# Experts stage: the two expert slots of a token are joined before the down-projection

## The reference, cut to what matters

```python
probs = softmax(x @ gate_w.T)                 # 8 experts
vals, idx = top_k(probs, 2)                   # two "slots" of each token
rw = vals / sum(vals)                         # weight of slot 0 and of slot 1
d1 = (x A1[e]) B1[e] * 2;  d3 = (x A3[e]) B3[e] * 2        # adapters of rank 16
act = silu(x w_gate + d1) * (x w_up + d3)     # per expert, 512 wide
out = (sum over e of weight * act) @ w_down.T
out = out + sum over e of weight * (act A2[e]) B2[e] * 2
```

## Time and profile before

| | |
|---|---|
| median of 3 runs | 1726.71 us (1726.4 to 1728.2) |
| time of the profiled execution | 1729.46 us |
| span of the profiled execution | 1727.7 us |
| PE busy | 1639.9 us (95%) |
| DVE busy | 1239.3 us (72%) |
| ACT busy | 926.0 us (54%) |
| POOL busy | 879.3 us (51%) |
| mean granted TensorE clock | 0.961 of full speed |

### The profile page before, as it was taken

The page is one execution under the profiler, slowest core; times in us unless marked ns, Lnnn a source line. Parts: engine busy times, 40 slices in busy tenths (PEclk is TensorE's granted clock), DMA queues, the critical chain, the costliest instruction groups (busy, mean ns, idle before and its releaser), DMA issues. The chain is left out here.

```text
span 1727.7 us, 42620 instructions
## 1 busy us (share of the span) xinstructions
PE 1639.9 (95%) x14336; PEld 1227.0 (71%) x14336; DVE 1239.3 (72%) x2888; ACT 926.0 (54%) x2189; POOL 879.3 (51%) x1006
## 2 busy tenths in 40 slices
PE   5999999999978999999999999897999999999998
PEld 2555555555545666666666666556999999999998
DVE  5887777777745767777676777536878788787876
ACT  3554444555533666666665666645554555455453
POOL 3544444444435767777766677622434334343442
PEclk9999999999977989999998999988999999999999
DMA  4000000000000000000000000000000000000000
GB/s 122 13 3 2 1 1 1 1 1 1 2 9 3 6 7 6 7 7 6 7 7 7 6 7 5 16 30 1 8 9 9 6 9 6 9 8 8 9 6 13
DMA packets 27869, 16.62 MB, mean 10 GB/s; under 512 B 6193, under 2 KB 25586, under 8 KB 27762
## 3 DMA queue, kind: packets, MB, share of 16 engines
q1 hardware_dynamic: 27762, 15.23, 3.2%
HBM read 9.97 MB, written 4.19 MB: 8 GB/s over the span
## 5 line engine op out<-in xcount | busy, mean ns | idle before, releaser
L323 ACT ACTIVATE sa_P<-sa_SK 128x1024 f32<-128x1024 f32 x128 | 131.2, 1025 | 149.0 <-PE sa_SK L514 149.0
L1554 POOL TENSOR_TENSOR ff_zz<-ff_zt 128x256 f32<-128x256 f32 x32 | 37.5, 1170 | 318.4 <-DVE ff_zt L1758 318.4
L278 POOL TENSOR_TENSOR sa_KM<-sa_HQK,sc_headmask 128x512 fp32r<-128x512 f32 x64 | 66.6, 1040 | 249.3 <-ACT sa_HQK L318 249.3
L963 ACT ACTIVATE xa_P<-xa_SK 77x1024 f32<-77x1024 f32 x128 | 130.1, 1016 | 95.0 <-PE xa_SK L1286 94.8
L1622 ACT ACTIVATE ff_SG<-bank 128x512 f32<-128x512 f32 x128 | 76.6, 598 | 188.7 <-PE bank L1835 188.7
L1748 DVE TENSOR_TENSOR ff_GL<-ff_GU,ff_GH 128x512 fp32r<-128x512 f32 x128 | 148.4, 1178 | 27.2 <-ACT ff_GH L1627 27.2
L408 DVE TENSOR_REDUCE sa_mx<-sa_SQ 128x8 f32<-128x1024 f32 x128 | 156.5, 1223 | 7.8 <-PE sa_SQ L514 5.4
L1900 PE MATMUL bank<-fh_r,ff_GH 128*128 128x256 f32 x512 | 149.3, 292 | 0.0
L889 POOL TENSOR_TENSOR xa_QMH<-xa_QBH,xc_headmask 128x512 fp32r<-128x512 f32 x64 | 72.6, 1134 | 148.0 <-ACT xa_QBH L953 147.9
L1833 PE MATMUL bank<-ff_ZH,fh_b 128*128 128x256 f32 x512 | 146.0, 285 | 0.0
L1902 PE MATMUL bank<-fh_r,ff_GL 128*128 128x256 f32 x512 | 144.5, 282 | 0.0
(11 more groups left out here) (259 smaller groups left out, 5394.7 us busy)
## 6 DMA issues: line engine op xcount, KB each, us to landing
xa_shift<-xa_row SPq DMA_DIRECT2D x256, 2.0 KB
out<-X SPq DMA_DIRECT2D x64, 64.0 KB, 1.5
cx<-ctx SPq DMA_DIRECT2D x64, 38.5 KB
sa_shift<-sa_mT SPq DMA_DIRECT2D x64, 8.0 KB, 1.8
X<-x SPq DMA_DIRECT2D x1, 768.0 KB, 6.4
xa_E<-L_ffn_B SPq DMA_DIRECT2D x2, 256.0 KB, 3.6
xa_E<-down_a SPq DMA_DIRECT2D x1, 512.0 KB, 4.3
X<-x SPq DMA_DIRECT2D x1, 256.0 KB, 2.9
```

The costliest lines, as they stand in the source:

```text
L323: nc.scalar.activation(P[:, 2 * (k % 2) + h, :], SK[:], ACT.Exp).then_inc(p_ready, 1)
L963: nc.scalar.activation(P[0:TC, (2 * b + h) % 4, :], SK[0:TC, :], ACT.Exp).then_inc(p_ready, 1)
```

## The change

Six edits, all within the experts:

1. **Slots joined.** The output is divided by the weight of slot 0: unit 2 and 3 (slot 1) are scaled by the ratio of the two weights, added to units 0 and 1, and only then split and projected down. POOL `scaled` multiplies the silu of slot 1 by the ratio; DVE `slot_sum` adds.
2. **The ratio.** DVE `odds` makes it, PE `ratios` spreads it over all 128 rows (two float32 matmuls of 128 columns), ACT `ratio_copy` brings it to the tile RB.
3. **Down-projection turned round.** `down` now has the weights stationary and 256 tokens as moving columns. The third adapter (bank PZ) is computed from slot 0's units and from the sums; the down-projection itself (bank OUT) from the sums alone.
4. **Masked adapter parts.** DVE `z_parts` masks the two with M0 - (M0 + M1) and M0 + M1, which POOL `output_masks` makes; ACT `z_hi` and DVE `z_lo` split both parts (128 by 512 in all), `extra` adds both to OUT. ACT `out_copy`, PE `back_T` and DVE `residual` bring the result back with tokens as rows.
5. **`x_lo` goes from DVE to POOL**, to the head of POOL's step. The comparisons in `ranks` become a function `compare` of two instructions instead of four, `second` and `slot_weights` go.
6. **Order.** New orders in `step` on PE, ACT, DVE and POOL, and the matching waits.

```diff
 @@ pool
-            def slot_sum(g):
-                pool.wait_ge(zt_done, NB * g + NB)
-                need(pool, zT_ps, g)
-                nc.gpsimd.tensor_tensor(zz[:], zt[:, :, 0, :], zt[:, :, 1, :], ALU.add).then_inc(zz_done, 1)
+            def slot_inputs(g, p, s):          # two of the four products as before, for one slot
...
+            def x_lo(g, p):
+                pool.wait_ge(xh_ready, g + 1)
+                need(pool, up_ps, UNITS * (g - 2) + 2)
+                nc.gpsimd.tensor_tensor(XX[1][:, p, :], xT[:], XX[0][:, p, :].bitcast(F32), ALU.subtract).then_inc(xl_ready, 1)
+            def output_masks(g, p):
+                pool.wait_ge(mask_sb, g + 1)
+                need(pool, zb_done, 2 * (g - 1))
+                nc.gpsimd.tensor_tensor(ME[:, p, 1], M[:, 0, :], M[:, 1, :], ALU.add).then_inc(me_done, 1)
+                pool.wait_ge(me_done, 2 * g + 1)
+                nc.gpsimd.tensor_tensor(ME[:, p, 0], M[:, 0, :], ME[:, p, 1], ALU.subtract).then_inc(me_done, 1)
+            def scaled(g, u):
+                pool.wait_ge(rb_sb, g + 1)
+                pool.wait_ge(silu_done, UNITS * g + 2 + u + 1)
+                unit2 = SG[:, u, :].rearrange("f (c n) -> f c n", c=2)
+                nc.gpsimd.tensor_tensor(unit2, unit2, RB[:].unsqueeze(1).to_broadcast([128, 2, NT]),
+                                        ALU.mult).then_inc(scaled_done, 1)
             def step(g, p):
-                if real(g - 1):
-                    slot_sum(g - 1)
                 if real(g + 1):
-                    slot_inputs(g + 1, 1 - p)
+                    x_lo(g + 1, 1 - p)
+                    slot_inputs(g + 1, 1 - p, 0)
+                scaled(g, 0)
+                scaled(g, 1)
+                if real(g + 1):
+                    slot_inputs(g + 1, 1 - p, 1)
+                    output_masks(g + 1, 1 - p)
 @@ act, step
                 if real(g + 1):
                     a_hi(g + 1)
+                ratio_copy(g)
...
                 silu(g, 2)
-                silu(g, 3)
                 if real(g - 1):
                     z_hi(g - 1)
-                g_hi(g, 2)
-                g_hi(g, 3)
+                silu(g, 3)
                 if real(g + 2):
                     input_T(g + 2, p)
+                g_hi(g, 2)
+                if real(g - 1):
+                    out_copy(g - 1)
+                g_hi(g, 3)
 @@ dve
+            def odds(g):
+                dve.wait_ge(w0_ready, g + 1)
+                nc.vector.reciprocal(w0_inv[:], W0[:, bass.ds(NB * g, NB)]).then_inc(inv_ready, 1)
+                dve.wait_ge(inv_ready, g + 1)
+                dve.wait_ge(w1_ready, g + 1)
+                need(dve, rb_ps, g)
+                nc.vector.tensor_tensor(ratio[:], w1[:], w0_inv[:], ALU.mult).then_inc(ratio_ready, 1)
             def gated(g, k):
-                dve.wait_ge(silu_done, UNITS * g + k + 1)
+                if k < 2:
+                    dve.wait_ge(silu_done, UNITS * g + k + 1)
+                else:
+                    dve.wait_ge(scaled_done, 2 * g + k - 1)
...
+            def slot_sum(g, u):
+                dve.wait_ge(gu_done, UNITS * g + 2 + u + 1)
+                nc.vector.tensor_tensor(GU[:, u, :], GU[:, u, :], G1[:, u, :], ALU.add).then_inc(sum_done, 1)
+            def z_parts(g, p):
+                dve.wait_ge(y_ps, UNITS * g + UNITS)
+                dve.wait_ge(me_done, 2 * g + 2)
+                need(dve, zh_done, g)
+                for part in range(2):
+                    nc.vector.tensor_tensor(zb[:, part, :], PZ[:, part * NT:(part + 1) * NT], ME[:, p, part],
+                                            ALU.mult).then_inc(zb_done, 1)
+            def residual(g):
+                dve.wait_ge(back_ps, g + 1)
+                for n in range(NB):
+                    xb = X[:, bass.ds((NB * g + n) * C, C)]
+                    nc.vector.scalar_tensor_tensor(xb, OUT[:, NT + n * C:NT + (n + 1) * C], W0[:, bass.ds(NB * g + n, 1)], xb,
+                                                   ALU.mult, ALU.add).then_inc(x_done, 1)
             def step(g, p):
+                odds(g)
+                if real(g + 1):
+                    compare(g + 1)
                 if real(g - 2):
-                    residual_z(g - 2)
+                    residual(g - 2)
                 if real(g + 1):
-                    x_lo(g + 1, 1 - p)
                     ranks(g + 1)
-                slot_weights(g, p)
                 gated(g, 0)
                 g_lo(g, 0)
                 if real(g + 1):
                     a_lo(g + 1)
                     picks(g + 1)
                 gated(g, 1)
-                if real(g - 1):
-                    slot_z(g - 1, 1 - p)
                 g_lo(g, 1)
                 if real(g - 1):
-                    residual_y(g - 1, 1 - p)
+                    z_parts(g - 1, 1 - p)
+                    z_lo(g - 1)
                 gated(g, 2)
+                slot_sum(g, 0)
                 gated(g, 3)
-                if real(g - 1):
-                    z_lo(g - 1)
+                slot_sum(g, 1)
                 g_lo(g, 2)
                 g_lo(g, 3)
 @@ pe
+            def ratios(g):
+                pe.wait_ge(ratio_ready, g + 1)
+                if real(g + 1):
+                    pe.wait_ge(route, ROUTE * (g + 1) + 1)
+                for n in range(NB):
+                    last = mm(BF[:, NT + n * T:NT + (n + 1) * T], ratio[:, n:n + 1].to_broadcast([128, 128]), ident[:],
+                              start=True, stop=True, skip_group_check=True)
+                last.then_inc(rb_ps, 1)
             def down(g, k):
...
+                    unit = [t[:, k, c * NT:(c + 1) * NT] for t in GG]
+                    at = k // 2 * NT
+                    last = three(PZ[:, at:at + NT], [t[:, f, C:2 * C] for t in RD], unit, f == 0, f == 3, skip_group_check=True)
+                    if k >= 2:
+                        last = three(OUT[:, 0:NT], [t[:, f, 0:C] for t in RD], unit, f == 0, False, skip_group_check=True)
+                for part in range(2):          # in extra(g)
+                    last = three(OUT[:, 0:NT], [t[:] for t in B2], [t[:, part, :] for t in ZP], False, part == 1,
+                                 skip_group_check=True)
             def step(g, p):
-                up(g, 0, p)
-                down(g, -2)
+                up_base(g, 0, p)
+                if real(g - 2):
+                    back_T(g - 2)
+                up_slot(g, 0, p)
+                down(g - 1, 2)
                 if real(g + 1):
                     a_products(g + 1, 1 - p)
-                up(g, 1, p)
-                down(g, -1)
+                ratios(g)
+                up_base(g, 1, p)
+                up_slot(g, 1, p)
                 if real(g + 1):
                     masks(g + 1)
-                up(g, 2, p)
-                up(g, 3, p)
-                if real(g - 1):
-                    z_T(g - 1)
-                down(g, 0)
+                down(g - 1, 3)
+                up_slot(g, 2, p)
+                up_slot(g, 3, p)
                 if real(g + 2):
                     input_T(g + 2)
+                down(g, 0)
                 down(g, 1)
+                if real(g + 2):
+                    logits(g + 2)
                 if real(g - 1):
                     extra(g - 1)
-                if real(g + 2):
-                    logits(g + 2)
```

More of the change, by code:

```diff
@@ L1443, in expert_ffn @@
     UNITS = 4
-    RANKED, ROUTE = 8, 13
+    RANKED, ROUTE = 6, 10
     ctx = ExitStack()
@@ L1550, in _ @@
         def _(pool):
-            def slot_sum(g):
-                pool.wait_ge(zt_done, NB * g + NB)
-                need(pool, zT_ps, g)
-                nc.gpsimd.tensor_tensor(zz[:], zt[:, :, 0, :], zt[:, :, 1, :], ALU.add).then_inc(zz_done, 1)
-            def slot_inputs(g, p):
-                pool.wait_ge(mask_sb, g + 1)
[L1558 to L1564, removed]
+            def slot_inputs(g, p, s):
+                pool.wait_ge(mask_sb, g + 1)
+                for part, done in enumerate((ah_done, al_done)):
+                    pool.wait_ge(done, g + 1)
+                    need(pool, up_ps, UNITS * (g - 2) + 2 * s + 2)
+                    nc.gpsimd.tensor_tensor(ZZ[part][:, p, s], AA[part][:].bitcast(F32),
+                                            M[:, s, :].unsqueeze(1).to_broadcast([C, 2, NT]),
+                                            ALU.mult).then_inc(z_done, 1)
@@ L1572, in _, with first @@
-            groups(pool, lambda: slot_inputs(0, 0), step, lambda: slot_sum(G - 1))
+                    x_lo(g + 1, 1 - p)
[5 more added lines that the diff above has]
+                    output_masks(g + 1, 1 - p)
+            def first():
+                x_lo(0, 0)
+                slot_inputs(0, 0, 0)
+                slot_inputs(0, 0, 1)
+                output_masks(0, 0)
@@ L1574, in _ @@
+            groups(pool, first, step, lambda: None)
         @block.scalar
@@ L1693, in a_lo, with compare @@
```

(26 more changed lines are left out.)

182 lines of the change are left out of this document (82 added, 100 removed).

## The result

The changed kernel takes 1954.28 us (median of 4, 1951.4 to 1958.12) against 1727.45 (1726.4 to 1733.04): 1.130 times as long, 95% interval 1.128 to 1.133. Slower was forecast, but by 116 us; it is 227, and the time lies outside the range. The page of the changed kernel, busy time and chain by line. PE is 1% of the chain, where it was 31%.

What follows compares the result with a forecast made beforehand. PE was taken to bound the kernel, the loop through the other engines 0.72 us behind. That loop becomes the period: 30 spacings of +3.73 us (+112), +3.1, +2.45 and -1 make +116.5, so 1843 us, range 1770 to 1900.

Steps and rivals of the forecast that it cites:

- what bounds the kernel before: Experts: PE sets the pace, without gaps at full clock, 16.72 us a group.
- the loop behind it: Mask copy, POOL's products, DVE, `spread`, `silu`, next mask copy: 16.00 us of 16.72, so 0.72 us of air.
- the first leg: From M (the group's mask copy ready) to DVE's last `g_lo`: 10.7 us after the change, for 6.91.
- Turns: DVE instructions with two SBUF inputs alternate with POOL products: five turns behind the mask copy, 0.45 us each.
- the second leg: From the last `g_lo` through DVE's start, `gated`, `picks`, `spread` and `silu` to the next mask copy: 9.75 us.
- a second new wait: PE's `a_products` waits for `x_lo` on POOL, 12.1 us after the mask copy; 1.6 us short of mattering.
- rival D: PE, no longer packed, loses full clock in the experts: 23 us a group, +195, about 1920 us; chance 0.13.
- PE's side: PE's own work for one group after the change, by count of matmuls: 15.87 us, for 16.72.
- the hold by `x_lo`: PE waits for `x_lo` on POOL ahead of `a_products`, but `spread` holds `silu` of unit 1 1.6 us longer.
- The sum: 30 group spacings of +3.73 us make +112, then +3.1, +2.45 and -1: +116.5, so 1843 us.

Runs made afterwards that it cites:

- experiment 4: Kernel before the change, with four extra DVE reductions of 512 resident elements at the head of DVE's step: 1768.55 us, 1.025.
- experiment 1: Changed kernel with DVE's `residual` moved one step earlier, behind the last `slot_sum`: 1831.85 us, 1.061 of the kernel before.
- experiment 3: Changed kernel with slot 1's gated product in its own PSUM bank, so `slot_sum` has one SBUF input: 1874.18 us, 1.086 of the kernel before.
- Experiment 7: Changed kernel with `residual` earlier, `slot_sum` reading its own PSUM bank, and ACT's mask copies ahead of `g_hi` of unit 1: 1780.06 us, 1.030.
- Experiment 2: Changed kernel with 30 unneeded matmuls in PE's gap ahead of `down` of unit 2: 1881.05 us, 1.089 of the kernel before.
- version 8: Changed kernel with `slot_sum` from PSUM, masks copied early, `x_lo` on POOL two groups ahead, and new POOL, ACT and DVE orders: 1768.57 us, 1.025.
- version 9: As version 8, with PE's `extra` and `back_T` earlier, `a_products` ahead of `down` of unit 2, ACT's `out_copy` behind `g_hi` 3: 1743.69 us, 1.0095.
- experiment 6: Changed kernel with `residual` one step earlier and `x_lo` back on DVE between `odds` and `compare`: 1825.01 us, 1.057 of the kernel before.
- experiments 5: Changed kernel with `residual` one step earlier and `slot_sum` reading its own PSUM bank: 1806.34 us, 1.048 of the kernel before.

## Why the prediction was wrong, step by step

**Right: what bounds the kernel before, and the length of the loop behind it.** The loop's 16.00 us and its 0.72 us of air were taken from rows, and experiment 4 bears them out to 0.4 us, though its chain does not pass through M and POOL. "Whatever lengthens it by more than that takes the pace from PE" is what happened.

**Right: the first leg.** M ready to the last `g_lo`: 10.7 worked out, 10.74 measured. Turns: the five instructions read 1.52, 1.03, 1.06, 1.78 and 1.21 us for 0.69 alone. `scaled`, the price that the trace before did not have, is 1.28 without a turn (experiment 1), as assumed. By the exclusive lock of the Trainium skill (SBUF — State Buffer, Who interferes with whom) a pair would take 1.94, an estimate; POOL's products with a turn start 1.69 and 1.70 us apart. The rule of the Trainium skill (SBUF — State Buffer, Who interferes with whom) that a DVE instruction with at most one SBUF input does not contend with GpSimd is what experiment 3 shows (0.69 and 1.28). Experiment 7 shows that M and POOL's row are in the loop now.

**Wrong: the second leg, the step "a second new wait".** The loop was closed through DVE's start, `gated`, `picks` and `spread`, at full clock. It closes through PE: `residual`, `down` of unit 2, unit 1's inputs, and for most of that at the half clock. The waits of PE were listed, and `down` of unit 2 was given to `g_lo` alone. Its other wait, for `residual`, was in the diff and not followed. At full clock it would have been the loop's longest branch: 10.74 + 2.27 + 5.6 + 2.53 = 21.1 us, against 20.45. (5.6 is 1.42 for `down`, 3.70 + 0.48 for what follows.) Experiment 2 measures that loop at 21.2; experiment 1, without the wait, 19.75. So the missed wait is 0.7 of the 3.5 us between forecast and result in the sum as it was written, and 1.5 against experiment 1. About 0.35 of that 1.5 is `residual`'s own time in DVE's start; without it the wait comes to about 1.1, an estimate from the 3.18 and 2.83 of experiment 1. The larger part, 2.7, is the clock, which the sum put at nothing.

**Wrong: rival D's price and chance.** The low clock was named as a rival at 0.13, because PE would still issue for most of the time. The mean share did not decide: in version 8 PE is busy 366 of the 400 us from 1250 to 1650 and the clock fell at times, in experiment 1 it is busy 342 of 400 and the clock stayed at 1.00. What differs is one single gap, of 1.5 us and more, in place of several of at most 1.05. The price was +2.6 us, on a path with 1.6 to spare; the missed wait took that air away, and the clock cost 2.7. The rival's 1920 us lies nearest to the result, in part by luck: it holds PE by `x_lo`, which in the changed kernel ends at 1687.73, 1.0 us before PE starts. The two errors meet: had the wait been seen, so would a gap of 4 us, from the end of `up_slot` to the end of `residual`. That the clock falls behind such a gap in the loop no row shown before the change told.

**Nearly right: PE's side.** One group's PE work was 15.87 by count. In version 9 PE is busy 385.10 of the 400 us from 1250 to 1650, which is 16.3 of its 16.95: 0.4 more than counted. Which matmuls make it is open.

**Right: the hold by `x_lo` is slack** (experiment 6), by the 1.04 us that PE still waits ahead of `masks` in experiment 1, where 1.6 was forecast.

**The sum.** Of the 7.2 us between the periods, 3.0 are the loop that was forecast at 3.7 (experiment 1), 1.5 the wait for `residual` with its own time on DVE (experiment 2 less 1), 2.7 the clock (result less experiment 2). In the two profiled spans the difference is 228.6 us: 212.4 in the 31 spacings of the mask copies (725.6 for 513.2 us), 10.7 behind the last copy, where +4.5 was forecast, and 5.5 ahead of the first, in the attention part and the experts' start. The 212.4 are less than 31 x 7.2, since the first three spacings are shorter in both kernels (14.26, 19.92 and 22.63 after; 13.53, 15.10 and 16.46 before).

## What to carry to other kernels

Before an edit to a kernel that one engine fills, close the loop through the other engines and write down its air; then put every wait of the bound engine's new queue into it, each `need` of the diff and not only those that hold data, since a wait for a bank to come free costs as much. Where such a wait opens a gap of more than a microsecond on TensorE, price the stretch behind the gap at the half clock too; a gap that cannot be closed may be worth filling with matmuls nobody needs (73 us here). Moving an element-wise product to GpSimd is not free while VectorE reads two SBUF operands beside it; with one of them in PSUM neither was slower here (0.69 and 1.28 us).

## What the runs showed of the hardware that was not expected

The granted clock fell to 0.50 once a group, behind a PE gap of 3.95 us, and stayed there for 5.9 us although PE was busy for all of it; behind gaps of 2.6 to 2.9 us it fell in about half of the groups (experiment 3), and behind gaps of 1.50 to 1.61 us in 6 of 29 (version 8), the shorter and the longer ones alike. Where the single waits were at most 1.05 us (experiment 1) or 1.33 us (experiments 5 and 7) it stayed at 1.00. 3.66 us of matmuls that nobody needs, put in the gap, removed the fall and 4% of the kernel's time.

A DVE product that reads one PSUM bank and writes its result back into the same bank took 0.70 us, as one that writes to SBUF (0.69).
